# VectorE's order in an attention layer: the reciprocals of the softmax sums and their spreading, moved ahead of two norms

## What is computed

```python
h = tok(x)                                   # softmax-weighted sum of the 4 views
h = h + attn(layernorm(h))                   # 16 heads of 16 channels, relative position bias
h = h + moe(layernorm(h))                    # 8 experts, hidden 1024, the best 2 for each token

def attn(x):
    q, k, v = split(x @ Wq.T), split(x @ Wk.T), split(x @ Wv.T)
    scores = einsum('bhqd,bhkd->bhqk', q, k) * 16 ** -0.5 + position_bias
    return (softmax(scores) @ v).merge_heads() @ Wo.T
```

## Time and profile before

| | us |
|---|---|
| median of 3 runs | 576.78 |
| lowest, highest | 576.09, 579.31 |
| the profiled execution | 578.61 |
| its span, first to last instruction | 576.6 |
| busy: TensorE | 510.0 |
| busy: TensorE's weight loads | 418.4 |
| busy: ScalarE | 267.3 |
| busy: VectorE | 236.8 |
| busy: GpSimd | 200.1 |

### The profile page before, as it was taken

One profiled execution on the slowest core, in us unless ns is written; L12 is line 12 of the kernel. 1 busy time (PEld: TensorE's weight loads), 2 busy tenths in 40 slices (PEclk: granted clock), 3 DMA queues, 4 the chain that ended last, 5 costly groups with the idle time before them and its releaser, 6 DMA issues.

```text
span 576.6 us, 13228 instructions
## 1 busy us (share of the span) xinstructions
PE 510.0 (88%) x3742; PEld 418.4 (73%) x3743; DVE 236.8 (41%) x1083; ACT 267.3 (46%) x1003; POOL 200.1 (35%) x186
## 2 busy tenths in 40 slices
PE   4689889999999999926999998999999999999980
PEld 3466556566556566615899997999999999999970
DVE  2777777787788777611222311111111111111110
ACT  1267687778877887712144332333333333333310
POOL 3131133323542552341333454333333333333221
PEclk9999999999999999966999999999999999999995
DMA  8890020203131131415666667566666666666615
GB/s 260 269 306 2 19 93 20 93 19 101 30 92 51 60 73 39 129 48 189 193 181 178 178 183 181 157 177 175 178 182 175 189 178 173 169 180 180 177 18 155
DMA packets 50999, 78.55 MB, mean 136 GB/s; under 512 B 10528, under 2 KB 39472, under 8 KB 50768
## 3 DMA queue, kind: packets, MB, share of 16 engines
q1 hardware_dynamic: 40160, 66.80, 36.0%
q0 software_dynamic: 8592, 10.58, 11.1%
q10 hardware_dynamic: 2208, 0.71, 0.6%
HBM read 68.27 MB, written 11.90 MB: 139 GB/s over the span
## 4 chain that ended last, share of the span: by engine, by line
PE 44%; DMA 5%; issue 2%; POOL 1%; DVE 1%; POOLq 0%; SPq 0%; DVEq 0%
PE psVO L974 21%; PE psS L962 12%; PE psP L962 10%; DMA fold<-xn_dram,sel 3%; DMA sum_dram<-fold,sel 2%; PE psQK L950 1%; DMA sel<-meta_dram 1%; POOL meta_dram L435 1%; POOL sum_dram L489 0%; POOLq L70 0%; DVE fold L1365 0%; PE psVO L846 0%; DVE fold L1361 0%; PE psG L877 0%; DVE fold L1356 0%
## 5 line engine op out<-in xcount | busy, mean ns | idle before, releaser
L974 PE MATMUL psVO<-xw,prob 128*128 x624 | 141.7, 380 | 0.8 <-DVE fold L1361 0.8
L974 PEld LDWEIGHTS psVO<-xw,prob 128*128 128x128 f32 x624 | 115.5, 190 | 15.6 <-issue 1.2
L489 POOL DMA_INDIRECT sum_dram<-fold,sel x39 | 61.8, 1583 | 169.2 <-DMA sel<-meta_dram 116.7
L589 ACT ACTIVATE prob<-prob,smin 128x128 f32<-128x128 f32 x256 | 99.5, 394 | 10.8 <-DVE smin L1140 9.1
L682 ACT ACTIVATE prob<-psS,b1T 128x128 f32<-128x128 f32 x160 | 45.5, 368 | 103.7 <-PE psS L962 98.7
L682 ACT ACTIVATE prob<-psP,b1T 128x128 f32<-128x128 f32 x152 | 43.2, 373 | 84.0 <-PE psP L962 80.2
L424 POOL TENSOR_TENSOR rstd<-ve,minus_half 128x1 f32<-128x1 f32 x32 | 32.7, 1020 | 139.7 <-DVE ve L1103 139.6
L962 PEld LDWEIGHTS psS<-fold,w1c 128*128 128x128 f32 x640 | 76.2, 196 | 1.9 <-DVE fold L1356 1.0
L962 PE MATMUL psS<-fold,w1c 128*128 128x128 f32 x640 | 76.8, 279 | 0.6 <-DVE fold L1356 0.6
L962 PEld LDWEIGHTS psP<-fold,w1c 128*128 128x128 f32 x608 | 70.7, 192 | 3.0 <-DVE fold L1356 2.1
L962 PE MATMUL psP<-fold,w1c 128*128 128x128 f32 x608 | 71.1, 275 | 1.8 <-DVE fold L1356 1.8
(11 more groups left out here) (165 smaller groups left out, 534.9 us busy)
## 6 DMA issues: line engine op xcount, KB each, us to landing
w1c<-in_L_ffn_W SPq DMA_DIRECT2D x39, 1024.0 KB
xw<-in_x SPq DMA_DIRECT2D x16, 512.0 KB, 8.1
xw<-in_L_ffn_W SPq DMA_DIRECT2D x8, 1024.0 KB
sum_dram<-h_all SPq DMA_DIRECT2D x17, 128.0 KB
xn_dram<-xn SPq DMA_DIRECT2D x16, 128.0 KB
out<-sum_dram SPq DMA_DIRECT2D x4, 512.0 KB, 5.6
relb<-in_L_ffn_b SPq DMA_DIRECT2D x1, 1024.0 KB
sel<-meta_dram SPq DMA_DIRECT2D x39, 2.0 KB
```

The costliest lines, as they stand in the source:

```text
L489: pool.indirect_dma_start(out=sum_dram.ap()[0:EARLY_B * S if j < EARLY else N_TOK + P, :], out_offset=bass.IndirectOffsetOnAxis(ap=row_no[ ...
L589: i = act.activation(blk, blk, ACT.Exp, bias=smin[:, k:k + 1], scale=-1.0, accum_out=ssum[:, k:k + 1])
L974: i = pe.matmul(psVO[:, 0:D], hT[u][:, c * P:(c + 1) * P], xw2[:, bass.ds(e * (HC * D) + c * D, D)], start=(c == 0), stop=(c == HC - 1))
```

## The change

In VectorE's `step`, `reciprocals` and `spread` of image `i - 1` are called right behind `residual`, ahead of `first_norm`, `rows` and `second_norm`. Before, `reciprocals` stood behind `rows` and `spread` behind `second_norm`. The instructions are the same, and no other engine's program is touched.

```diff
                 if late:
                     residual(i - 2)
+                if back:
+                    reciprocals(i - 1, 1 - u)
+                    spread(i - 1)
                 if nxt:
                     first_norm(i + 1)
                 if place is not None:
                     rows(place)
-                if back:
-                    reciprocals(i - 1, 1 - u)
                 if late:
                     second_norm(i - 2)
-                if back:
-                    spread(i - 1)
                 if gate is not None:
                     masks(gate)
```

## The result

| | before | after |
|---|---|---|
| median, us | 578.25 (5 runs, 576.09 to 579.31) | 570.63 (5 runs, 570.45 to 571.64) |
| ratio | | 0.9876, interval 0.9855 to 0.9898 |
| span of the profiled execution, us | 576.6 | 569.8 |

The kernel is 1.2% faster: 7.2 us by the ratio (the two medians are 7.6 us apart). The forecast was a gain of 2.6 us and a time of 574.2 us.

The account below looks back on a forecast made before the run. The loop from TensorE's projections over VectorE's residual, norms, spread and biased scores to ScalarE's exponentials and `x1T` was taken to bound the steps. Gain 1.9 + 0.8 + 0.2 - 0.3 = 2.6 us: 574.2 us, range 571.0 to 577.5.

Parts of the forecast that it names:

- ScalarE closes the step, TensorE's wait is a side branch: Normal steps: the loop runs through VectorE and ScalarE's exponentials to `x1T`; TensorE's 0.69 us idle is partly lost there.
- Term (a): Normal steps: biased scores start at most 0.27 us earlier; 0.04 or 0.19 us left, by whether GpSimd or VectorE goes first.
- Term (b): Normal steps: the copy of `x2T` waits for TensorE's transposes; as these come earlier, 0.13 us a step go.
- The sign that I was wrong: Steps shorter by over 0.5 us would mean that ScalarE is not on the loop.
- Steps 2 and 3: Step 2, closed by TensorE and VectorE, gains 0.65 to 1.0 us, taken as 0.8; step 3 counted as normal, 0.24.
- Mask steps: Two steps with masks: only the earlier biased scores count, 0 to 0.27 us each, taken as 0.1, 0.2 together.
- Steps with `rows`: Three steps: TensorE never waited for `srcw` and a later `rows` is covered, so 0 us.
- Last step: TensorE's 10.36 us of idle time are hidden by the chain of scatter, records and gather: 0 us.
- step 15: Positions ready some 0.55 us later, so the final chain starts 0.1 to 0.6 us later: 0.3 us taken as cost.
- The slower one: Where the spread meets the end of `kbd`, `rstd` is pushed behind copies and first norm: 582.9 us, chance 0.10.
- Nothing: Another link of the loop is the tight one, only the cost near the end is left: 577.1 us, chance 0.15.
- The full return of TensorE's wait: ScalarE not on the loop, 10.3 us in 11 steps return: 566.8 us; full or a larger return, chance 0.15.

Follow-up runs that it names:

- the two one-sided kernels: Changed kernel with two extra copies behind the second norm: ratio 0.9925; changed kernel with TensorE's `srcw` transposes held for a one-column copy behind that norm: ratio 0.9953.
- the second profile of the changed kernel: Changed kernel run once more without an edit, against the kernel before: ratio 0.9896 (0.9863 to 0.9929).
- step 15 alone: Kernel before with the new order in step 15 only: ratio 0.9995 (0.9974 to 1.0015).

## Why the prediction was right or wrong, point by point

- *ScalarE closes the step, TensorE's wait is a side branch.* Right, shown by the two one-sided kernels (12.87 and 13.03 to 13.10 us a step) and by TensorE's wait for `x1T`, which grew from 2.9 to 8.5 us. Of 10.3 us of wait in 11 steps 1.35 are left, in steps 2 and 3, and 5.7 us came back as shorter steps.
- *Term (a), the start of the biased block.* The mechanism was right, the size was not. I had 0.27 us at most and gave 0.04 to 0.19, since the copies might lose the tie with `rstd` at the end of `kbd`. The tie went to VectorE: `rstd` took 0.62 us in place of 0.59 (0.69 in step 6), the copies 0.44 in place of 0.36, the first norm 0.40 in place of 0.65. 0.25 us were gained in a normal step, close to the most. Two figures of that working are slightly off: 0.27 less 0.1 leaves 0.17 and not 0.19, and a first norm that ends at 101.38 and costs `rstd` 0.02 us says that `rstd` needs the shared part at 101.36, not 101.33. Neither changes the forecast by more than 0.1 us.
- *Term (b), behind TensorE.* This is the step that failed, in "a normal step": I stopped at the copy of `x2T` (0.13 us, measured 0.12 to 0.13) and took the exponentials behind it to follow for their own reasons. They waited 0.22 to 0.24 us more for the biased block 1, that is for TensorE's scores. The rows that show it, 105.75 in ScalarE's timeline and 104.69 in VectorE's, I left out of the sum, although 0.48 us between a copy of 0.37 us and the next instruction were there to be seen. I reckoned ScalarE as having "hardly a gap", since 0.37 + 4 x 0.40 fills 1.97 of 2.04 us; but these durations overlap (each next start is 0.25 us behind the copy's and 0.38 behind an exponential's), so the sum hid the gap.
- Together a normal step gave 0.61 us and not 0.24. The link that I left out is there in all of them, steps 4 and 13 too, which gave only 0.29 (0.05 by (a), none by (b), 0.24 by that link) and 0.47 us (0.10, 0.13, 0.24).
- *The sign that I was wrong.* I had written that steps shorter by over 0.5 us mean that ScalarE is not on the loop. They came out shorter by 0.61 us, and ScalarE is on it all the same: the sign was drawn from a sum that lacked a link.
- *Steps 2 and 3.* The selection of the other images in step 2 (L744) starts 15.15 us behind the `x1T` copy that opens this step, in place of 16.19: 1.04 us earlier, which is the upper end of 0.65 to 1.0, where I took 0.8. By the `x1T` copies 0.61 us of it fall in step 2. The other 0.43 us fall in step 3, whose first norm hangs on that selection; with 0.63 us from the three links they make its 1.06. I had counted step 3 as a normal one: its wait was 2.08 us, the longest of all in these 11 steps, and I did not look at it by itself.
- *Mask steps.* There are three (6, 10 and 14), not two; I had put the first among the normal ones. They gave 0.17, 0.43 and 0.25 us against 0.1: right in kind, since the copy of `x2T` and the exponentials behind it follow as closely before (1.55 and 0.25 us) as after, so neither (b) nor the link that I left out has a part there.
- *Steps with `rows`.* 0, right, as was step 1.
- *Last step.* Right that its 10.36 us are hidden: nothing from the order of that step. Most likely wrong in sign on step 15, where I charged 0.3 us and the profiles give about 1 us, though no time tells it from nothing. The sign that I had named, a chain that moves by over 1 us, was just met (36.90 and 35.88 us). The shifts that I worked out came (first scatter 0.59 us later, `W2` 0.14 us later), and the pair behind them landed earlier all the same.
- *The rivals.* The slower one falls with `rstd` at 0.62 us, where 0.86 was its turning point. "Nothing" falls. The full return of TensorE's wait falls too, but the gain of 7.2 us lies nearer to its 10.0 than to my 2.6. The Trainium skill's rule on the shared port pair (SBUF — State Buffer, Terms) is borne out in kind by the stretched copies and the shortened first norm. Its "full instruction" is not what the recorded lengths show: in most steps the copies are stretched by 0.08 us and `rstd` by 0.03 us. In steps 2 and 3, where the copies come well ahead of the end of GpSimd's `kbd`, they take 0.86 us in place of 0.36, and TensorE still waits 0.42 and 0.93 us for them.

The sum as the two first profiles have it: 5.7 us in the steps and 1.0 us in the last stretch make 6.7 us. The times give 7.2 us in the first comparison and 6.0 us in the second (ratio 0.9896).

## What to carry to other kernels

An engine's wait is worth what the loop that closes the step gives back, and every link of that loop has to be followed to its end: here three separate links lay behind one instruction, and I priced two. Look for gaps by the starts of consecutive instructions, not by adding their durations, because durations overlap. Work that can fill a wait (here two copies in the time of an `rstd`) should stand in that wait, ahead of the instruction that waits and not behind it; how far ahead matters much less.

## What was not expected of the hardware

- Four indirect scatters in a row, in place of two and a wait, made ScalarE and VectorE stand still for 2.3 to 3.0 us in the steps of this kernel. At the end of the phase, where eight go out in two fours, it is there too (1.88 and 2.44 us behind the first four), but the time did not rise.
- The second pair of scatters could go out 0.3 to 1.2 us earlier (17.0 to 17.4 us behind the `x1T` copy in place of 17.8 to 18.2) in kernels whose first pair went out 0.6 us later.
- Single steps take longer in some profiles, without a row that names a cause: step 1 by 2.25 us in the second profile of the changed kernel, step 3 by 1.4 us in that of step 15 alone (18.21 us in place of 16.80).
- Which of two engines starts first can be worth 0.4 us a step. GpSimd's `rstd` of the first norm takes 1.48 to 1.62 us in nearly every step, when VectorE's half of `kbd` has started just ahead of it (97.73 and 97.88 in the step of the earlier trace rows). In step 10 of the second profile of the changed kernel it came first:

```profile
162.91 0.56 POOL L424 TENSOR_TENSOR rstd<-ve,minus_half 128x1 f32<-128x1 f32 x1 [0.87 <-DVE ve L1103]
...
163.03 1.23 DVE L259 TENSOR_TENSOR kbd<-qkT,hmask 128x1024 f32<-128x1024 f32 x1
```

It took 0.56 us, and the step 12.84 us in place of 13.25. No run here puts it first in every step.
